# Cross-attention of a two-layer perceiver block: values and turned probabilities as bf16 parts, output turned in pairs, statistics from a second load, context normalized by ScalarE

## The reference

```python
xn = layer_norm(x, gamma); ctx = layer_norm(context, ctx_gamma)   # context: 16 x 1601 x 512
q = (xn @ Wq).reshape(b, n, 16, 64).transpose(0, 2, 1, 3) * scale
k, v = split(ctx @ Wkv)                       # one head of 64 for all 16 query heads
sim = where(mask == 0, -inf, q @ k.T)
out = (softmax(sim) @ v).reshape(b, n, 1024) @ Wout
out = out + silu(gate) * a @ Wff2             # h = xn @ Wff1, split in a, gate
...
gamma = mean(abs(W)) + 1e-6                   # of W_fc and W_proj: 16 x 128 rows of 512 each
```

## Time and profile before

| | |
|---|---|
| median of 3 runs | 1466.77 us |
| profiled execution: span from the first to the last instruction | 1461.7 us |
| the runs' median less that span | 5.1 us |
| TensorE busy | 1345.7 us (92%), 11070 matmuls |
| VectorE busy | 923.3 us (63%) |
| ScalarE busy | 557.2 us (38%) |
| GpSimd busy | 502.5 us (34%) |
| mean granted TensorE clock | 0.959 |
| cross-attention, feed-forward, output products end near | 423, 590, 720 us |

### The profile page before, as it was taken

The page is one execution under the profiler, slowest core; times in us unless marked ns, Lnnn a source line. Parts: engine busy times, 40 slices in busy tenths (PEclk is TensorE's granted clock), DMA queues, the critical chain, the costliest instruction groups (busy, mean ns, idle before and its releaser), DMA issues.

```text
span 1461.7 us, 28439 instructions
## 1 busy us (share of the span) xinstructions
PE 1345.7 (92%) x11070; PEld 810.3 (55%) x11070; DVE 923.3 (63%) x2273; ACT 557.2 (38%) x1149; POOL 502.5 (34%) x424
## 2 busy tenths in 40 slices
PE   6889999999999999999999879989798998879998
PEld 3458888888864444444445545444345455655554
DVE  6858888888743323500657785766997467676761
ACT  3446777777762222000133326133313244233430
POOL 3003100000048335734416220343770049995300
PEclk9979999999999999999999979999999999779999
DMA  6112232221112111311000100211330001110000
GB/s 187 39 49 64 81 102 75 65 66 58 52 44 87 57 57 58 73 57 57 30 30 30 60 30 1 80 37 59 115 123 1 1 2 59 60 59 1 1 22 37
DMA packets 50429, 79.19 MB, mean 54 GB/s; under 512 B 13808, under 2 KB 14320, under 8 KB 50304
## 3 DMA queue, kind: packets, MB, share of 16 engines
q1 hardware_dynamic: 47296, 70.83, 15.3%
q0 software_dynamic: 1920, 6.29, 1.4%
q10 hardware_dynamic: 1088, 0.37, 0.1%
HBM read 75.38 MB, written 2.10 MB: 53 GB/s over the span
## 4 chain that ended last, share of the span: by engine, by line
PE 70%; DVE 22%; issue 4%; ACT 4%; DMA 1%; SPq 0%; DVEq 0%; ACTq 0%
PE psum L635 40%; PE psum L968 7%; PE psum L877 5%; PE psum L1292 4%; PE psum L644 4%; PE psum L867 2%; DVE big L2212 2%; PE psum L980 1%; DVE stats L2183 1%; DVE big L1971 1%; PE psum L860 1%; PE psum L650 1%; PE psum L861 1%; PE psum L1280 1%; DVE big L2026 1%
## 5 line engine op out<-in xcount | busy, mean ns | idle before, releaser
L2961 POOL TENSOR_TENSOR ring_hi<-stage,small 128x512 bf16<-128x512 f32 x128 | 140.7, 1100 | 610.7 <-DVE big L2228 371.1
L635 PE MATMUL psum<-y_mem,ring_hi 128*128 128x512 bf16 x896 | 270.2, 384 | 5.9 <-DVE y_mem L2384 2.0
L635 PE MATMUL psum<-ring_hi,y_mem 128*128 128x512 bf16 x576 | 174.1, 388 | 6.2 <-DVE ring_lo L2541 3.3
L635 PE MATMUL psum<-y_mem,ring_lo 128*128 128x512 bf16 x448 | 171.7, 383 | 0.0
L2964 POOL TENSOR_TENSOR ring_lo<-stage,ring_hi 128x512 bf16<-128x512 f32 x128 | 154.4, 1207 | 10.0
L1414 ACT ACTIVATE big<-psum 128x400 bf16<-128x400 f32 (+2 forms) x232 | 124.1, 547 | 81.8 <-PE psum L635 40.0
L635 PEld LDWEIGHTS psum<-y_mem,ring_hi 128*128 (+1 forms) x896 | 87.0, 99 | 108.5 <-issue 9.5
L635 PE MATMUL psum<-ring_lo,y_mem 128*128 128x512 bf16 x352 | 117.5, 386 | 0.0
L1414 ACT ACTIVATE y_mem<-psum 128x512 bf16<-128x512 f32 x64 | 37.1, 596 | 182.6 <-PE psum L644 182.2
L635 PEld LDWEIGHTS psum<-ring_hi,y_mem 128*128 128x128 bf16 x576 | 57.0, 100 | 73.1 <-issue 9.7
L2310 DVE TENSOR_TENSOR side<-psum,ybuf 128x512 f32<-128x512 f32 x32 | 22.1, 692 | 108.3 <-ACT ybuf L1641 108.3
(11 more groups left out here) (260 smaller groups left out, 2835.3 us busy)
## 6 DMA issues: line engine op xcount, KB each, us to landing
big<-in_ctx_dram SPq DMA_DIRECT2D x64, 200.0 KB
stage<-in_L_xattn_Wff_dram SPq DMA_DIRECT2D x12, 1024.0 KB, 5.3
ybuf<-in_L_ffn_W_fc_dram SPq DMA_DIRECT2D x16, 256.0 KB, 2.7
ybuf<-in_L_ffn_W_proj_dram SPq DMA_DIRECT2D x16, 256.0 KB, 3.0
stage<-in_L_ffn_W_fc_dram SPq DMA_DIRECT2D x4, 1024.0 KB, 5.2
stage<-in_L_ffn_W_proj_dram SPq DMA_DIRECT2D x4, 1024.0 KB, 5.2
stage<-in_L_xattn_Wout_dram SPq DMA_DIRECT2D x3, 1024.0 KB, 5.2
stage<-in_L_attn_W_qkv_dram SPq DMA_DIRECT2D x3, 1024.0 KB, 5.3
```

Of the source, the lines that this page charges most:

```text
L635: ins = pe.matmul(bank, l, r, start=n == 0, stop=n == len(passes) - 1)
L2961: pool.tensor_tensor(hi[:, k], src[:, k], zero, ALU.add).then_inc(pool_part, 1)
```

## The change

1. *Values and probabilities as parts.* ScalarE's copies of the turned probabilities and of the values of the keys become bf16 high parts; VectorE subtracts the low parts (`low_p` at the end of each step, `values_low` in step 7), and `values` becomes a `product` of three bf16 passes for each of the 4 tiles. It waits for the low part.
2. *Output turned in pairs.* `turn_out` turns two heads at a time (4 transposes for a batch and not 8, in step 2), one high and one low copy each. The queries are stored in another order to fit (`q_place`).
3. *Statistics from a second load.* Each context tile is loaded once more into `ybuf`, and VectorE's statistics are taken there, at the times of the list `stat_at`, one tile at a time; the inverse roots come in six groups of batches. The instructions of a chain no longer wait one by one but before the next of the chain.
4. *Context normalized by ScalarE* (`ctx_normed`, scale and bias a column) and no longer by VectorE.
5. *Signs.* Mask and keys are stored negated, the maximum becomes a minimum of negated scores, and the exponential has scale -1; the sign change instruction goes.
6. *Banks.* The extras take banks 5, 6 and 7 in turn; each waits until the one three before is read.
7. *Order.* Context tiles are turned one a step in steps 0 to 3 and their low parts are taken one a step in steps 1 to 4, the mask row comes in step 1, the turned output in 2.
8. *Sums of the weights* leave the steps: ScalarE issues the loads and sums them behind the feed-forward, and their total moves on VectorE behind the first heads of the self-attention.

The diff, cut to its core:

```diff
+        SIDE_BANKS = (5, 6, 7)
+        side_order, side_bank = [], {}
+
+        def side_freed(key):
+
+            kind, n = key
+            return {"t": ("ctx_lo", n + 1), "m": ("mask_copied", n + 1), "k": ("k_lo", n + 1), "v": ("v_lo", n + 1),
+                    "o": ("ot_lo", n + 1)}[kind]
+
+        STAT_GROUPS = ((0, 1), (1, 2), (2, 4), (4, 8), (8, 12), (12, 16))
+        group_of = {b: q for q, (b0, b1) in enumerate(STAT_GROUPS) for b in range(b0, b1)}
+        stat_at = [(-2, 0)] * 4 + [(-1, 0)] * 4 + [(0, 0)] * 4 + [(0, 1)] * 4
+        stat_at += [(0, j) for j in range(4, 8) for _ in range(2)] + [(1, j) for j in range(8)]
+        stat_at += [(b, j) for b in (2, 3, 4, 5, 6, 7, 8, 9) for j in range(4, 8)]
+        assert len(stat_at) == TAIL_TILES * B
+        newton_at = {0: 2, 2: 3, 6: 4, 10: 5}
...
+                def side(kind, n):
+                    key = kind, n
+                    at = len(side_order)
+                    side_order.append(key)
+                    side_bank[key] = SIDE_BANKS[at % len(SIDE_BANKS)]
+                    if at >= len(SIDE_BANKS):
+                        x_wait(pe, *side_freed(side_order[at - len(SIDE_BANKS)]))
+                    return psum[:, side_bank[key], :]
...
-                    x_wait(pe, "p_copied", max(g - 1, 0))
+                    x_wait(pe, "p_lo", max(g - 1, 0))
...
                 def values(g):
                     b, j = divmod(g, 8)
                     if j == 0:
-                        x_wait(pe, "v_copied", b + 1)
+                        x_wait(pe, "v_lo", b + 1)
                         x_wait(pe, "o_norm", b)
-                    x_wait(pe, "p_copied", g + 1)
-                    for kt in range(TAIL_TILES):
-                        ins = pe.matmul(O_BANK[:, j * XD:(j + 1) * XD], v["PT"][0:R, g % 2, kt, :], v["V"][b % 2][0:R, kt, :],
-                                        start=kt == 0, stop=kt == TAIL_TILES - 1)
+                    x_wait(pe, "p_lo", g + 1)
+                    ins = product(O_BANK[:, j * XD:(j + 1) * XD],
+                                  [(cut(v["PT"], lambda x: x[0:R, g % 2, kt, :]),
+                                    tuple(v["V"][b % 2][0:R, kt, x, :] for x in range(2))) for kt in range(TAIL_TILES)])
                     ins.then_inc(XN["pv"], 1)
...
+                def turn_out(b):
+                    bank = side("o", b)
                     x_wait(pe, "o_norm", b + 1)
...
+                    for jp in range(4):
+                        ins = pe.transpose(bank[:, jp * P:(jp + 1) * P], v["O"][:, 2 * jp:2 * jp + 2, :].rearrange("p j d -> p (j d)"),
+                                           ident[:])
                     ins.then_inc(XN["ot_ready"], 1)
...
-                    if j in (0, 2) and b + 1 < B:
+                    if j < 4 and b + 1 < B:
                         turn_ctx(b + 1, j)
-                        turn_ctx(b + 1, j + 1)
-                    if j in (1, 5) and b:
-                        turn_out(b - 1, j // 5)
-                    if j == 3 and b + 1 < B:
+                    if j == 1 and b + 1 < B:
                         mask_row(b + 1)
+                    if j == 2 and b:
+                        turn_out(b - 1)
                     if j == 4 and b + 1 < B:
                         keys(b + 1)
                     if j == 6 and b + 1 < B:
                         values_of_keys(b + 1)
                 values(STEPS - 1)
-                for half in range(2):
-                    turn_out(B - 1, half)
+                turn_out(B - 1)
...
+                def ctx_normed(b, kt):
+                    t = 4 * b + kt
+                    act.wait_ge(ctx_in[kt], 16 * (b + 1))
+                    act.wait_ge(rstd_ready, group_of[b] + 1)
+                    tile = v["ctx"][0:R, kt]
+                    act.activation(tile, tile, ACT.Identity, bias=v["nw"][0:R, 0, t:t + 1], scale=v["nw"][0:R, 1, t:t + 1])\
+                        .then_inc(XN["ctx_norm"], 1)
...
+                ctx_normed(1, 0)
                 for g in range(STEPS):
                     b, j = divmod(g, 8)
                     if g + 1 < STEPS:
                         exp(g + 1)
+                    if b == 0 and j < 3:
+                        ctx_normed(1, j + 1)
                     copy_p(g)
-                    if j in (0, 2) and b + 1 < B:
+                    if j < 4 and b + 1 < B:
                         ctx_high(b + 1, j)
-                        ctx_high(b + 1, j + 1)
-                    if j in (1, 5) and b:
-                        out_high(b - 1, j // 5)
-                    if j == 3 and b + 1 < B:
+                    if j == 1 and b + 1 < B:
                         mask_rows(b + 1)
+                    if j == 2 and b:
+                        out_high(b - 1)
                     if j == 4 and b + 1 < B:
                         keys_high(b + 1)
                     if j == 6 and b + 1 < B:
                         values_of_keys(b + 1)
-                    if j == 7:
-                        weight_sums(b)
-                for half in range(2):
-                    out_high(B - 1, half)
-                x_wait(act, "g_summed", B)
+                    if j >= 4 and b + 2 < B:
+                        ctx_normed(b + 2, j - 4)
+                out_high(B - 1)
...
+            def load_rows(r):
+                act.dma_start(ybuf[:, r % 2], (fc_rows, proj_rows)[r % 2][r // 2]).then_inc(rows_loaded[r % 2], 16)
+
+            load_rows(0)
+            load_rows(1)
+            for r in range(2 * B):
+                act.wait_ge(rows_loaded[r % 2], 16 * (r // 2 + 1))
+                act.activation(ybuf[:, r % 2], ybuf[:, r % 2], ACT.Abs, accum_out=gsum[:, r % 2, r // 2:r // 2 + 1]).then_inc(rows_summed, 1)
+                if r + 2 < 2 * B:
+                    act.wait_ge(rows_summed, r + 1)
+                    load_rows(r + 2)
...
+                def tile_stats():
+                    t = taken[0]
+                    taken[0] += 1
+                    if t % 4 == 0:
+                        due()
+                    dve.wait_ge(stat_in[t % 2], 16 * (t // 2 + 1))
+                    dve.bn_stats(stats[0:R, t % 4, :], ybuf[0:R, t % 2]).then_inc(stat_used, 1)
+                    if t % 4 == 3:
+                        dve.wait_ge(stat_used, t + 1)
+                        for u in range(4):
+                            ins = dve.bn_aggr(v["mv"][0:R, t - 3 + u, :], stats[0:R, u, :])
+                        later(ins)
...
+                def values_low(b):
+                    x_wait(dve, "v_copied", b + 1)
+                    bank = psum[0:R, side_bank["v", b], 0:TAIL_TILES * XD].rearrange("p (t e) -> p t e", e=XD)
+                    dve.tensor_tensor(v["V"][b % 2][0:R, :, 1, :], bank, v["V"][b % 2][0:R, :, 0, :], ALU.subtract).then_inc(XN["v_lo"], 1)
...
-                    dve.tensor_tensor_reduce(v["P"][:, g % 2, :], psum[:, g % 2, 0:n_keys], v["mb"][i], 1.0, NEG, ALU.add, ALU.max,
-                                             xq_max[:, i, j:j + 1]).then_inc(max_step, 1)
-                    dve.wait_ge(max_step, g + 1)
-                    dve.tensor_scalar(xq_neg[:, i, j:j + 1], xq_max[:, i, j:j + 1], -1.0, None, ALU.mult).then_inc(XN["s_max"], 1)
+                    dve.tensor_tensor_reduce(v["P"][:, g % 2, :], psum[:, g % 2, 0:n_keys], v["mb"][i], 1.0, -NEG, ALU.add, ALU.min,
+                                             xq_neg[:, i, j:j + 1]).then_inc(XN["s_max"], 1)
+
+                def low_p(g):
+                    x_wait(dve, "p_copied", g + 1)
+                    hi, lo = (x[0:R, g % 2] for x in v["PT"])
+                    dve.tensor_tensor(lo, psum[0:R, 2 + g % 2].rearrange("p (t q) -> p t q", q=P), hi, ALU.subtract).then_inc(XN["p_lo"], 1)
...
                 for g in range(STEPS):
                     b, j = divmod(g, 8)
+                    if j == 0:
+                        roots = inverse_roots(newton_at[b]) if b in newton_at else iter(())
+                        sums = iter(())
                     if j == 5 and b + 1 < B:
                         keys_low(b + 1)
                     if g + 2 < STEPS:
                         maximum(g + 2)
-                    if j == 0:
-                        if b:
-                            out_normed(b - 1)
-                        if b + 1 < B:
-                            ctx_normed(b + 1, 2)
-                            ctx_normed(b + 1, 3)
-                    if j in (1, 3) and b + 1 < B:
+                    if j == 7:
+                        sums = inverse_sums(b)
+                        some(sums, 1)
+                    if b or j > 1:
+                        some(roots, 2)
+                    if j == 0 and b:
+                        out_normed(b - 1)
+                    if 1 <= j <= 4 and b + 1 < B:
                         ctx_low(b + 1, j - 1)
-                        ctx_low(b + 1, j)
-                    if j in (2, 6) and b:
-                        out_low(b - 1, j // 6)
-                    if j == 4:
```

(75 more changed lines are left out.)

241 lines of the change are left out of this document (119 added, 122 removed).

## The result

The changed kernel takes 1496.3 us (median of 4 runs, 1492.2 to 1497.5), the kernel before 1466.7 (4 runs, 1459.8 to 1467.0): ratio 1.0207 (95% interval 1.018 to 1.0234), 29.5 us slower, where 21 were forecast. The profiled executions have spans of 1493.7 and 1461.7: 32.0 us between them. (In the runs that have both on record, a time lies some 1.8 us over its span, 1495.5 for 1493.7 here. So the profiled execution of the kernel before was probably one of some 1463.5 us, 3 under the median, and most of the prediction's 5.1 us around the span is that; the forecast difference of 21 does not use them.) The traces divide the 32.0 us as follows. The context keys' product of TensorE marks the batches.

A forecast was written before the change was run, and what follows sets the result against it. TensorE was taken to bound the batch now, the round with VectorE after the change. 13.3 + 8 x 0.7 - 5 x 0.4 + three root-link batches at 0.7 + 2.4 - 0.4 = 21 us, so 1466.8 + 21 = 1488; range 1456 to 1514.

The forecast's parts named there:

- Values: Cross-attention, TensorE: 12 bf16 passes replace four f32 products, 0.35 us a step for 0.84.
- Rival D: Values product: loads of 100 rows are slow, 0.055 us more a pass, kernel at 1508; chance 0.08.
- The round: Cross-attention: values wait for VectorE's low part, the next turn and maximum behind them; 21.3 us a batch, 0.7 more.
- Rival B: Cross-attention: VectorE is the bound without the round, but for keys and their values; kernel 1464 or 1458; chance 0.18.
- E: Cross-attention: TensorE's side gains as claimed and the rest hides, 70 us gained, kernel at 1397; chance 0.03.
- ScalarE: Cross-attention: ScalarE's work about 14.3 us a batch, with context normalizations at 0.5 each; not the bound.
- Batches 0 and 1: Start of the cross-attention: second loads through two buffers, low clock and batch 1's statistics cost 13.3 us together.
- the 3 us for the low clock in steps 2 to 4: Batch 0: TensorE's clock is at 0.50, which makes steps 2 to 4 3 us longer.
- Root links: Three cross-attention batches with square-root links on VectorE: 0.7 us more each.
- Rival C: Cross-attention: TensorE, 68% busy, drops to the low clock; a quarter of the time costs 28 us, kernel 1515; chance 0.14.
- The sum over the weights: Ahead of the self-attention: moved sum delays bias row and first row maximum by 2.4 us, bounds 1 and 4.
- the late batches: Batches 10 to 14, statistics done: steps 5 and 7 shorter by 0.1 and 1.0, 20.2 us a batch, 0.4 less.

The follow-up runs named there:

- Experiment 1: Values product queued a step later on TensorE, output's normalization moved to VectorE's step 1, against the changed kernel: 1474.6 us.
- experiment 6: Context low parts taken one step earlier on VectorE, on top of the changed kernel with values product a step later: 1455.9 us; on the changed kernel alone: 1476.9 us.
- experiment 3: Sum over the weights' row sums and its signal put back before the output's norms, against the changed kernel: 1494.9 us.
- experiment 9: 17 idle products put ahead of TensorE's wait for the sum over the weights, against the changed kernel: 1504.9 us.
- experiment 8: Values product later, context low parts earlier, six load buffers and weights' sum moved back, against the changed kernel: 1437.6 us, again 1439.2; without the sum moved back 1443.4.

## Why the prediction was right, and where it was off

*Values.* 0.35 a step: held. The 12 passes have weights of 100 rows and still go at 0.34 / 12 = 0.028 us. Rival D falls. The Trainium skill has the rule that a weight load's time goes by its columns, whatever its rows, in another section of the page than the prediction names (TensorE: Matmul & The Clock Gate, LDWEIGHTS (loading the stationary operand)). The 0.028 us agrees with it.

*The round.* Held, step by step within 0.17 us, in sum 21.19 against 21.3. Experiment 1 shows the cause for the steps that wait for the values product, experiment 6 for steps 2 and 4. Rival B (VectorE's own work alone) and E fall with them: VectorE works 16.3 us of a batch (16.6 forecast), and the rest is wait.

*ScalarE.* 14.3 us a batch forecast, 15.2 measured: the context's normalization takes 0.80 us, and the next instruction starts 0.70 after its start, where 0.5 was put, with 0.63 as the upper bound. That bound was the exponential's, of 400 columns; this one has 512, with a scale and a bias column:

```profile
L1579 ACT ACTIVATE big<-big x64: 798/804/813, 68.5 to 413.6; 100x512 f32<-100x512 f32 x64
```

In batches 2 to 9 it hides. In 10 to 14, where the statistics no longer fill VectorE's time, VectorE waits 1.6 us for three high parts that ScalarE copies late behind the normalization. So step 5 keeps its 2.40 and step 7 falls to 2.00, where 2.2 and 1.8 were forecast, and these batches take 20.55, not 20.2.

*Batches 0 and 1.* The sum was near, the terms were not. Step 0 of batch 1 opens at 132.59; 129.1 plus 3 for the clock was forecast. The term that was too small is the landing, put at 2.5 us within 2.0 to 3.1. A pair of second loads is issued at 97.36, 101.80 and 105.49 us, and the statistic that waits for it starts at 101.08, 104.67 and 108.97: 3.7, 2.9 and 3.5 us from issue to use. The first wait for loads is 4.29 us:

```profile
97.36 0.73 SPq L2969 DMA_DIRECT2D ybuf<-in_ctx_dram  x2
95.51 1.28 DVE L2241 BATCH_NORM_STATS2 stats<-ybuf 100x6 f32<-100x512 f32 x2
101.08 1.39 DVE L2241 BATCH_NORM_STATS2 stats<-ybuf 100x6 f32<-100x512 f32 x2 [4.29 <-DMA ybuf<-in_ctx_dram]
108.97 0.69 DVE L2241 BATCH_NORM_STATS2 stats<-ybuf 100x6 f32<-100x512 f32 x1 [2.82 <-DMA ybuf<-in_ctx_dram]
132.59 0.57 DVE L2299 CUSTOM_DVE_ANT_0 big<-psum,side 128x400 f32<-128x400 f32 x1
```

Steps 0 and 1 took 8.4 and 8.1 us (6.7 and 7.0 forecast), step 7 4.5 (3.4), while the 3 us for the low clock in steps 2 to 4 did not show: 9.9 us together, as their own work. Batch 1 took 23.4 for 23.0. After it comes the next term.

*Root links.* This step failed in size: 0.7 us each was forecast over the plain batch, and 4.2, 1.0 and 1.6 came. The 1.0, in the batch whose clock is 1.00 throughout (234.15 to 256.31), is the price of the links themselves. The 4.2 has two more causes, and the forecast had neither. The first is GpSimd, which works on weight tiles beside batch 2:

```profile
157.78 1.05 DVE L2264 TENSOR_TENSOR big<-big 100x16 f32<-100x16 f32 x1
157.75 1.04 POOL L3076 TENSOR_TENSOR ring_hi<-stage,small 128x512 bf16<-128x512 f32 x1 [14.30 <-DVE big L2324]
246.73 0.17 DVE L2264 TENSOR_TENSOR big<-big 100x16 f32<-100x16 f32 x1
```

The same link takes 0.17 us in batch 6, where GpSimd rests. Here it ends with the GpSimd instruction beside it, and step 0 takes 3.36 us for 2.48; three more links of this batch take 0.53 to 0.65. In the traces of the changed kernel and of the experiments all 32 such links (TENSOR_TENSOR, 100x16) of over 0.3 us end 0.03 us after the end of a GpSimd instruction that they overlap; no run takes GpSimd away. The second cause is the clock. The low part comes late, TensorE idles 1.84 us ahead of the values product at 159.57, and then the granted clock falls, which the forecast did not chain to it (columns as in the first windows row):

```profile
156.00:160.00 4.00, 2.10 (x35) 1.77 (x36) 3.90 (x13) 2.03 (x5) 2.17 (x2) 1.00 0.35 101
160.00:164.00 4.00, 3.74 (x30) 2.68 (x27) 3.38 (x11) 2.33 (x6) 3.69 (x5) 0.57 0.20 55
164.00:168.00 4.00, 3.67 (x28) 3.14 (x29) 2.51 (x8) 2.09 (x6) 3.05 (x3) 0.57 0.16 51
```

How the 4.2 divides between the two no run shows. Rival C did not come as a whole: the mean clock from 130 to 423 us is 0.98, and it is 1.00 in the plain batches with TensorE at 76%. But its mechanism acts in places: 0.57 for 8 us here, 0.92 over the third batch with links (22.74), and in experiment 6 in five batches that have no links. Which stretches it hits differs between executions, and with it the time by some us: the batch that takes 22.16 here took 24.92 in experiment 3, and the one that takes 22.74 here took 22.16 there.

*The sum over the weights.* The reorder was found, and the bias row starts where it was put (788.42, against 762.4 + 26.0). The term was mis-sized, 5.0 for 2.4 and beyond its bound of 4: 1.7 of the 2.6 are the clock after 3.86 us of idleness (experiment 9), the rest lies in what follows the row. ScalarE's 32 row sums took from 617.17 to 687.34, 70.2 us for 70, and hid, as forecast.

*The rest*: -1.1 up to the last head copy was not forecast and is not explained. The +1.1 after the row maximum is less than what two executions of one kernel differ by there (3.9 us, experiment 8).

*Near for mixed reasons.* The mechanism was right, and the direction with it. Of the 11 us by which the traces' 32.0 exceed the forecast 21, the root links are 4.6, the sum's place 2.6, batches 0 and 1 2.0 and the late batches 1.8. All four were put too low.

## What to carry to other kernels

When an operation moves from one engine's surplus to a hand-over, ask what stands behind it in the consumer's queue: a cheap product behind a late operand delays everything queued after it, and the work saved never appears. Issue the consumer one step later before judging the arithmetic. Then look for a second order that holds the same loop: here there were two, each worth 1.8 us a batch. A buffer pair that covers a steady loop does not cover a start in which four tiles are wanted in one step. A stall on TensorE can cost its length and then slow passes after it (3.86 us idle, then 1.7 us lost). And when a batch takes what was forecast, read its granted clock before calling the forecast right: 20.5 us in experiment 6 were 19.44 of order and 1.1 of clock.

## Unexpected of the hardware

ScalarE's activation of 100x512 f32 in place with a scale and a bias column takes 804 ns in the median of 64 (798 to 813), while its plain copy of 100x512 from PSUM takes about 0.58 us. TensorE after 3.86 us of idleness took 0.41 to 0.43 us a pass of 512 columns for eight passes (788.63 to 792.03), at the lower of its two clock levels, and then 0.22; with products in the idle stretch every pass took 0.22. A link of 100x16 on VectorE, 0.17 us by itself, took up to 1.05 us beside a GpSimd instruction and ended with it. The same loop, instruction for instruction, took 26.65 or 28.28 us in batch 1 depending on the execution (mean granted clock from 90 to 170 us 0.79 and 0.73). And a clock fall can come back in batch after batch: in experiment 6 it stands at 282.9 us in batch 8 and at 303.4 in batch 9, a batch of 20.5 apart, with TensorE idle for 1.2 us just before.
